# Selective scan in a Trainium2 kernel: one state's input tile of sixteen moved from TensorE to VectorE

## The chip, the core and the metric

The kernel runs on one core of one Trainium2 chip. The metric is the device time of one execution in microseconds (us). The core's engines have queues of their own and work side by side; they wait for one another with semaphores: TensorE (PE in the profile, its weight loads are PEld), VectorE (DVE), ScalarE (ACT), GpSimd (POOL) and SyncE (SP), which issues the DMA transfers. TensorE writes only to PSUM; VectorE and ScalarE can reach PSUM, GpSimd works in SBUF.

## The reference, cut

The program is four layers deep (a Mamba layer with a selective scan, a gated expert layer, a second Mamba-like mixer, a quantised feed-forward layer), with layer norms and residuals between them. The change touches the scan of the first:

```python
def _selective_scan(x, dt, A, Bm, Cm):        # 4 sequences, 1024 channels, 256 steps, 16 states
    def step(h, inp):
        x_t, dt_t, B_t, C_t = inp
        dA = jnp.exp(dt_t[..., None] * A)
        dBx = dt_t[..., None] * B_t[:, None, :] * x_t[..., None]
        h = dA * h + dBx
        y = jnp.einsum('bdn,bn->bd', h, C_t)
        return (h, y)
```

For each state n, h is a first-order recurrence over time with decay exp(dt.A[n]) and input dt.x.B[n]; y is the sum over n of h.C[n]. B and C are the same for all channels.

## The kernel before, in words

`selective_scan` (from L472) lays channels on the 128 partitions and time on the free axis. A unit is one state n of a "pair": two tiles of 128 channels (`a` = 0, 1) by one half of the tokens (512, two sequences), so 1024 elements a partition. There are 2 halves x 4 pairs x 16 states = 128 units; unit i is pair `kk` = i // 16 and state `n` = i % 16. For each unit:

- ScalarE, `decay(i)` (L540): da = exp(dt.A[n]), two instructions of 510 columns. Two buffers: it waits for scan i-2 (`s_h`).
- TensorE, `inputs(i)` (L669): the tile dt.x.B[n] into a PSUM buffer `dbx[i % 2]`. B[n] varies with time, which lies on the free axis. So u = dt.x is turned once a pair (`turn`, L648; `copied`, L551, takes it to SBUF as `uT`), and eight 128x128 matmuls of `uT` with a diagonal matrix of B[n] (`diag`) turn it back and scale it. It waits for scan i-2.
- VectorE, `scan(i)` (L600): the recurrence, from da (SBUF) and dbx (PSUM), into one of three buffers `hh`. It waits for da, dbx and for GpSimd's product i-3.
- GpSimd (L635 on): pr = h.C[n], with C[n] a row that was broadcast to all partitions (`crow`, four states a DMA, L529). It waits for scan i, and for `summed(i-3)`, which frees its buffer.
- TensorE, `summed(i)` (L690): eight transposes of pr that add up in PSUM `zT`. It waits for the product i.

TensorE's queue is written out by hand (L702 on): in iteration i it holds `inputs(i+2)`, then `turn(kk+1)` at n = 10, then `summed(i-2)`, then `turn_back(kk-1)` at n = 5. ScalarE's queue is `decay(i)`, and after it `summed_out(kk-1)` at n = 4 (copies zT to u), `copied(kk+1)` at n = 13 and, in pair 3, `narrow_diag` (L564), which makes the diagonal of the second half. `summed(0)` of the next pair starts zT anew and so waits for `summed_out`. VectorE's queue is the scans in order, with `skip(kk-1)` (L608) behind scan 8 and `dt_x(kk+1)` (L592, u = dt.x) behind scan 9. The first diagonals are made by `wide_diag` (L514), four by VectorE and six by GpSimd, the last six by ScalarE.

SyncE sends the C rows to DRAM in `scan_front` (L287) and loads them broadcast in `selective_scan` (L524 to L529), for the second half when the last pair of the first half has used them.

Of the kernel before, what the change touches and what calls it, by code (L numbers as in the profile page):

```python
# [15 lines left out]
F32 = mybir.dt.float32  # L16
F32R = mybir.dt.float32r
ALU = mybir.AluOpType
ACT = mybir.ActivationFunctionType
AX_X = mybir.AxisListType.X  # L20

P = 128
BATCH, SEQ, DM = 4, 256, 512
TOK = BATCH * SEQ
MT = TOK // P
KD = DM // P
HALF = 512
# [5 lines left out]
DIN, NST, RNK, TAPS = 1024, 16, 32, 4  # L33
CD = DIN // P
NX = RNK + 2 * NST
SCAN_EPS = 1e-6

NE, ER = 8, 16
# [44 lines left out]
def build(nc, I, out):  # L83

    with ExitStack() as top:
# [22 lines left out]

        x_tok = I["x"].rearrange("(m p) d -> p m d", p=P)
        out_tok = out.rearrange("(m p) d -> p m d", p=P)  # L110
        c_dram = nc.dram_tensor("c_rows", [NST, TOK], F32, kind="Internal").ap()
        acs_dram = nc.dram_tensor("acs_rows", [NHEAD, TOK], F32, kind="Internal").ap()
        tab_dram = nc.dram_tensor("step_tables", [NG, P, 3 * MT * 2 * PAIRS], F32, kind="Internal").ap()
        x_dram = nc.dram_tensor("x_kept", [TOK, DM], F32, kind="Internal").ap().rearrange("(m p) d -> p m d", p=P)
# [116 lines left out]
def scan_front(nc, sem, sb, banks, I, xT, xc, sz, dt, bt, cst, eps, c_dram, o):  # L231

    R = RNK + 2 * NST
# [3 lines left out]
    with ExitStack() as c:  # L237
# [33 lines left out]
        with nc.Block() as block:  # L271
            @block.sync
            def _(sp):
                def load(s):
                    if s >= 2:
                        sp.wait_ge(s_lo, s - 1)
                    sp.dma_start(ws[s % 2][:], I["w_in0"][s]).then_inc(s_w[s % 2], 16)

                load(0)
                load(1)  # L280
                for t, n in ((cw, "conv_w0"), (cb, "conv_b0"), (xp, "x_proj"), (dp, "dt_proj"), (db, "dt_bias0"),
                             (lw, "ln_w0")):
                    sp.dma_start(t[:], I[n]).then_inc(s_tab, 16)
                for s in range(2, CD):
                    load(s)
                sp.wait_ge(s_bcn, 2)
                sp.dma_start(c_dram, bcn[RNK + NST:R, :]).then_inc(s_out, 16)  # L287
                sp.wait_ge(s_out, 16)

            @block.gpsimd  # L290
            def _(pool):
# [180 lines left out]
def selective_scan(nc, sem, sb, banks, I, xc, dt, o, bt, ident, c_dram):  # L472
# [8 lines left out]
    BR = 4  # L481
    with ExitStack() as c:
        crow = sb(c, "ss_c", [P, NST, HALF])
        diag = sb(c, "ss_diag", [P, NST, TB, P])
        na = sb(c, "ss_na", [P, CD, NST])
        dd = sb(c, "ss_d", [P, CD])
        u = sb(c, "ss_u", [P, 2, HALF])
# [13 lines left out]
        s_zs, s_zt = sem("ss_zT_copied"), sem("ss_z_turned_back")  # L501
        s_dbx, s_da, s_h, s_pr, s_y, s_fin = (sem("ss_dbx_ready"), sem("ss_decay"), sem("ss_h_ready"), sem("ss_prod"),
                                              sem("ss_summed"), sem("ss_done"))
        V_FIRST, P_FIRST = 4, 10
        two = lambda t: t.rearrange("p (a t) -> p a t", a=2)

        def tokens(kk):
            half = kk // PR
# [4 lines left out]

        def wide_diag(eng, n):  # L514

            return eng.tensor_tensor(diag[:, n], ident.unsqueeze(1).to_broadcast([P, TB, P]),
                                     bt[:, 0:TB, n].unsqueeze(2).to_broadcast([P, TB, P]), ALU.mult)

        with nc.Block() as block:
            @block.sync  # L520
            def _(sp):
                sp.dma_start(na[:], I["a_log0"]).then_inc(s_in, 16)
                sp.dma_start(dd[:], I["d_0"]).then_inc(s_in, 16)
                for half in range(NH):  # L524
                    for r0 in range(0, NST, BR):
                        if half:
                            sp.wait_ge(s_pr, UNITS // NH - NST + r0 + BR)
                        src = c_dram[r0:r0 + BR, half * HALF:(half + 1) * HALF]
                        sp.dma_start(crow[:, r0:r0 + BR, :], src.partition_broadcast(P)).then_inc(s_c[r0 // BR], 16)  # L529

            @block.scalar
            def _(act):
# [18 lines left out]
                def copied(kk):  # L551
                    act.wait_ge(s_ut, kk + 1)
                    if kk >= 2:
                        act.wait_ge(s_dbx, (kk - 1) * NST)
                    for a in range(2):
                        act.activation(uT[kk % 2][:, a].rearrange("p m d -> p (m d)"), tz[:, a * HALF:(a + 1) * HALF],
                                       ACT.Copy).then_inc(s_us, 1)

                def summed_out(kk):
                    act.wait_ge(s_y, (kk + 1) * NST)  # L560
                    for a in range(2):
                        act.activation(u[:, a, :], zT[:, a * HALF:(a + 1) * HALF], ACT.Copy).then_inc(s_zs, 1)

                def narrow_diag(half, n):  # L564
                    for m in range(TB):
                        ins = act.activation(diag[:, n, m, :], ident, ACT.Copy,
                                             scale=bt[:, half * TB + m, n:n + 1])
                    ins.then_inc(s_dact, 1)

# [5 lines left out]
                for i in range(2, UNITS):  # L575
                    kk, n = divmod(i, NST)
                    decay(i)
                    if n == OUT_AT and kk:
                        summed_out(kk - 1)
                    if n == TURN_AT + 3 and kk + 1 < KB:  # L580
                        copied(kk + 1)
                    if kk == PR - 1:
                        act.wait_ge(s_dbx, i + 1)
                        narrow_diag(1, n)
                summed_out(KB - 1)

# [1 line left out]
            def _(dve):  # L588
# [3 lines left out]
                def dt_x(kk):  # L592
                    if kk >= 2:
                        dve.wait_ge(s_zt, kk - 1)
                    elif kk:
                        dve.wait_ge(s_ut, kk)
                    dve.tensor_tensor(u[:], dt[:, tiles(kk), tokens(kk)], xc[:, tiles(kk), tokens(kk)], ALU.mult
                                      ).then_inc(s_u, 1)

                def scan(i):  # L600
                    dve.wait_ge(s_da, i + 1)
                    dve.wait_ge(s_dbx, i + 1)
                    if i >= RH:
                        dve.wait_ge(s_pr, i - RH + 1)
                    dve.tensor_tensor_scan(hh[i % RH], da[i % 2][:], dbx[i % 2][:], 0.0, ALU.mult, ALU.add  # L605
                                           ).then_inc(s_h, 1)
# [9 lines left out]

                dt_x(0)
                for n in range(V_FIRST):
                    wide_diag(dve, n).then_inc(s_dv, 1)
                dve.wait_ge(s_in, 32)  # L620
                for i in range(UNITS):
                    kk, n = divmod(i, NST)
                    scan(i)
                    if n == SKIP_AT and kk:
                        skip(kk - 1)
                    if n == TURN_AT - 1 and kk + 1 < KB:
                        dt_x(kk + 1)
# [19 lines left out]
            def _(pe):  # L647
# [20 lines left out]

                def inputs(i):  # L669
                    kk, n = divmod(i, NST)  # L670
                    if i >= 2:
                        pe.wait_ge(s_h, i - 1)
                    if kk == 0:
                        if n < V_FIRST:
                            pe.wait_ge(s_dv, n + 1)
                        elif n < P_FIRST:
                            pe.wait_ge(s_dp, n - V_FIRST + 1)
                        else:
                            pe.wait_ge(s_dact, n - P_FIRST + 1)
                    if kk == PR:  # L680
                        pe.wait_ge(s_dact, NST - P_FIRST + n + 1)
                    for a in range(2):
                        if n == 0:
                            pe.wait_ge(s_us, 2 * kk + a + 1)
                        for m in range(TB):
                            ins = pe.matmul(dbx[i % 2][:, a * HALF + m * P:a * HALF + (m + 1) * P], uT[kk % 2][:, a, m, :],  # L686
                                            diag[:, n, m, :], start=True, stop=True)
                    ins.then_inc(s_dbx, 1)

                def summed(i):  # L690
# [1859 lines left out]
```

## Time and profile before

| | |
|---|---|
| median of 3 runs | 2571.89 us (2567.72 to 2571.96) |
| the profiled execution | 2572.07 us, its span 2570.3 us |
| busy in the span | PE 2378.4, PEld 1923.2, DVE 1840.6, ACT 1504.5, POOL 1213.2 us |
| L605, the scans | 128, 291.5 us busy, 2283 ns each |
| L686, `inputs` | 2048 matmul records (16 a unit), 253.7 us busy |
| L642, the products by C | 128, of 2401 and 2395 ns mean |
| L597, `dt_x` | 8, 12.4 us busy, 1547 ns each |

The scan stage runs from the first scan at 187.1 us to the last at 546.8 us. All times in the rows are microseconds from the start of the span, a row's duration is its second number. The releaser in brackets is what ended the idle time of the engine before the row. Each `inputs` is 8 matmul instructions and shows as 16 records of loads and of matmuls, each `summed` as 8. PEclk is the granted clock of TensorE, 1.00 at 2.4 GHz and 0.50 at 1.2 GHz. Starts and ends of neighbouring rows can overlap by some hundredths, since ends are modelled.

### The profile page before, as it was taken

The page shows a single profiled execution, that of the slowest core. Times are in us where ns is not written, and L with a number is a line of the kernel's source. Part 1 is how long each engine was busy: PE and PEld are TensorE (multiplying, and loading weights), DVE is VectorE, ACT ScalarE, POOL GpSimd, SP SyncE. Part 2 cuts the span into 40 slices and gives each one's busy share as a digit, 9 for nine tenths or more (in the row PEclk, how much of TensorE's full clock was granted, in tenths as well). Part 3 has the DMA queues.
Part 4 walks back from the last instruction along what each step waited for, and adds up shares of the span by engine and source line. Part 5 has one row for each costly group of instructions (what it writes and reads, how often), then busy time and mean ns, then how long its engine had stood idle before and what let it go on. Part 6 is the DMA issues. An engine that isn't in the chain of part 4 may idle for free. (4 is left out here: it accounts for less than half of the span.)

```text
span 2570.3 us, 38269 instructions
## 1 busy us (share of the span) xinstructions
PE 2378.4 (93%) x13836; PEld 1923.2 (75%) x13836; DVE 1840.6 (72%) x3052; ACT 1504.5 (59%) x3201; POOL 1213.2 (47%) x782
## 2 busy tenths in 40 slices
PE   5979999977659999999999999999999999779997
PEld 4559999976446777777777777777777777569996
DVE  4558888874537866866866966857857857597777
ACT  2355584553327966956956857867857768632221
POOL 1228888864224643633634625724625535432212
PEclk9989999988869999999999999999999999889999
DMA  2010020021022412322312312313312213201100
GB/s 83 26 61 7 1 66 2 1 70 34 30 86 88 124 58 79 110 65 77 119 50 80 113 54 92 97 58 99 94 60 96 87 62 99 92 25 50 41 35 34
DMA packets 108541, 167.42 MB, mean 65 GB/s; under 512 B 9489, under 2 KB 77457, under 8 KB 107329
## 3 DMA queue, kind: packets, MB, share of 16 engines
q1 hardware_dynamic: 108352, 164.97, 20.2%
q8 instruction: 111, 1.82, 0.3%
q14 instruction: 78, 0.63, 0.1%
HBM read 158.58 MB, written 6.36 MB: 64 GB/s over the span
## 5 line engine op out<-in xcount | busy, mean ns | idle before, releaser
L78 PE MATMUL mg_pb<-xTh,mg_wh 128*128 128x512 f32 x1152 | 479.5, 416 | 16.7 <-POOL mg_wl L1525 16.7
L1535 POOL TENSOR_TENSOR mg_y<-mg_hT,mg_sg 128x512 f32<-128x512 f32 x128 | 187.8, 1467 | 598.2 <-DVE mg_hT L1771 598.2
L79 PE MATMUL mg_pb<-xTl,mg_wh 128*128 128x512 f32 x1152 | 453.7, 394 | 0.0
L80 PE MATMUL mg_pb<-xTh,mg_wl 128*128 128x512 f32 x1152 | 452.3, 393 | 0.0
L1719 DVE SCALAR_TENSOR_TENSOR mg_hT<-mg_pb,mg_cw,mg_hT 128x510 f32<-128x510 f32 (+2 forms) x432 | 318.8, 742 | 31.4 <-ACT mg_hT L1891 22.7
L605 DVE TENSOR_TENSOR_SCAN o<-ss_da,ss_dbx 128x1024 f32<-128x1024 f32 x128 | 291.5, 2283 | 53.6 <-PE ss_dbx L686 48.9
L1746 DVE TENSOR_TENSOR mg_m<-mg_gb,mg_cb 128x384 f32<-128x384 f32 x512 | 265.7, 550 | 71.6 <-ACT mg_gb L1941 68.2
L78 PEld LDWEIGHTS mg_pb<-xTh,mg_wh 128*128 128x128 f32 x1152 | 217.3, 189 | 75.9 <-issue 19.2
L686 PE MATMUL ss_dbx<-ss_diag,ss_uT 128*128 128x128 f32 x2048 | 253.7, 278 | 8.6 <-DVE o L605 7.6
L548 ACT ACTIVATE ss_da<-dt,ss_na 128x510 f32<-128x510 f32 x256 | 170.3, 714 | 146.3 <-DVE o L605 146.1
L80 PEld LDWEIGHTS mg_pb<-xTh,mg_wl 128*128 128x128 f32 x1152 | 217.2, 189 | 51.3
L686 PEld LDWEIGHTS ss_dbx<-ss_diag,ss_uT 128*128 128x128 f32 x2048 | 241.7, 194 | 11.2 <-DVE o L605 10.0
L79 PEld LDWEIGHTS mg_pb<-xTl,mg_wh 128*128 128x128 f32 x1152 | 218.0, 189 | 38.5
L642 POOL TENSOR_TENSOR ss_pr<-o,ss_c 128x1024 f32<-128x1024 f32 x86 | 206.4, 2401 | 37.1 <-PE ss_zT L697 34.5
L1941 ACT ACTIVATE mg_gb<-mg_nd 128x256 f32<-128x256 f32 x512 | 189.8, 371 | 54.7 <-DVE mg_nd L1764 54.7
L1935 ACT ACTIVATE mg_gb<-mg_abc,mg_tabs 128x128 f32<-128x128 f32 x512 | 183.3, 358 | 22.8 <-DVE mg_m L1746 21.7
L1525 POOL TENSOR_TENSOR mg_wl<-mg_ws,mg_wh 128x1024 fp32r<-128x1024 f32 x72 | 177.5, 2465 | 6.0
L78 PE MATMUL mg_tb<-mg_wogh,mg_yh 128*128 128x512 f32 x448 | 180.0, 402 | 0.0
L79 PE MATMUL mg_tb<-mg_wogl,mg_yh 128*128 128x512 f32 x448 | 177.1, 395 | 0.0
L80 PE MATMUL mg_tb<-mg_wogh,mg_yl 128*128 128x512 f32 x448 | 177.0, 395 | 0.0
L1621 PE MATMUL mg_py<-mg_m,mg_hc 128*64 128x256 f32 x1024 | 165.6, 402 | 9.6 <-DVE mg_m L1746 9.5
L1795 DVE SCALAR_TENSOR_TENSOR o<-mg_tb,mg_rs,o 128x512 f32<-128x512 f32 x56 | 41.8, 747 | 179.5 <-PE mg_tb L80 179.5
(321 smaller groups left out, 5387.3 us busy)
## 6 DMA issues: line engine op xcount, KB each, us to landing
mg_abc<-acs_rows SPq DMA_DIRECT2D x256, 256.0 KB, 3.4
mg_ws<-in_w_in SPq DMA_DIRECT2D x72, 512.0 KB, 3.6
mg_wos<-in_w_out SPq DMA_DIRECT2D x64, 256.0 KB, 3.7
ss_c<-c_rows SPq DMA_DIRECT2D x8, 1024.0 KB, 5.7
ff_ws<-in_w SPq DMA_DIRECT2D x7, 1024.0 KB, 4.8
x<-in_x SPq DMA_DIRECT2D x16, 256.0 KB, 4.2
ip_ws<-in_w_in SPq DMA_DIRECT2D x8, 512.0 KB, 3.5
ff_w2s<-in_w SPq DMA_DIRECT2D x7, 512.0 KB, 5.8
```

Source lines behind the costliest of these rows:

```text
L78: pe.matmul(out, lhs[0], rhs[0], start=start, stop=False)
L79: pe.matmul(out, lhs[0], rhs[1], start=False, stop=False)
L80: return pe.matmul(out, lhs[1], rhs[0], start=False, stop=stop)
L605: dve.tensor_tensor_scan(hh[i % RH], da[i % 2][:], dbx[i % 2][:], 0.0, ALU.mult, ALU.add).then_inc(s_h, 1)
L642: pool.tensor_tensor(pr[i % RP], two(hh[i % RH]), crow[:, n, :].unsqueeze(1).to_broadcast([P, 2, HALF]), ALU.mult).then_inc(s_pr, 1)
L686: ins = pe.matmul(dbx[i % 2][:, a * HALF + m * P:a * HALF + (m + 1) * P], uT[kk % 2][:, a, m, :], diag[:, n, m, :], start=True, stop=True)
L1525: pool.tensor_tensor(wl[s % 2][:], ws[:], wh[s % 2][:].bitcast(F32), ALU.subtract).then_inc(s_lo, 1)
L1535: pool.tensor_tensor(yb[:, p % RING, t], hT[s % 2][:, t], sg[s % 2][:, t], ALU.mult).then_inc(s_y2, 1)
L1719: i = dve.scalar_tensor_tensor(out=d3, in0=s3, scalar=w[:, TAPS - 1 - k:TAPS - k], in1=d3, op0=ALU.mult, op1=ALU.add)
L1746: dve.tensor_tensor(mm[u % 4][:], gb[u % 2][:, 0:BLK], cbt[:, u // 2, :], ALU.mult).then_inc(s_m, 1)
L1935: act.activation(gb[u % 2][:, 2 * P:BLK], abc[(BATCH * p + b) % 3][:, hh, P:SEQ], ACT.Exp, bias=tabs[g % 2][:, 2, 2 * b, 2 * q + hh:2 * q ...
L1941: act.activation(gb[u % 2][:, 0:2 * P], nd[u % 4][:], ACT.Exp, scale=1.0 if by_dve(p, b) else -1.0).then_inc(s_e, 1)
```

## The change

State 2 of each pair (`BY_DVE`) gets its tile from VectorE. VectorE multiplies u (dt.x, still in SBUF and not turned) by a row of B[2] that is broadcast to all partitions (`brow`), and writes the product into the same PSUM buffer that TensorE would have used. The instruction is queued behind scan 0 of the pair; it waits for that scan, and in pairs 0 and 4 for the row's DMA. `scan(2)` waits for it. TensorE's `inputs` returns at once for state 2 and the other 15 states stay as they are, with their counts of semaphores moved (`at`, `by_pe`). There is one diagonal fewer. SyncE writes one more row to DRAM in the front, and loads `brow` ahead of the C rows of each half. `summed_out` waits for the product too, since it overwrites u.

```diff
+BY_DVE = 2
-                sp.dma_start(c_dram, bcn[RNK + NST:R, :]).then_inc(s_out, 16)
-                sp.wait_ge(s_out, 16)
+                sp.dma_start(c_dram[0:NST, :], bcn[RNK + NST:R, :]).then_inc(s_out, 16)
+                sp.dma_start(c_dram[NST:NST + 1, :], bcn[RNK + BY_DVE:RNK + BY_DVE + 1, :]).then_inc(s_out, 16)
+                sp.wait_ge(s_out, 32)
...
-        diag = sb(c, "ss_diag", [P, NST, TB, P])
+        diag = sb(c, "ss_diag", [P, NST - 1, TB, P])
+        brow = sb(c, "ss_b", [P, HALF])
-        V_FIRST, P_FIRST = 4, 10
+        V_FIRST, P_FIRST = 5, 10
+        def at(n):
+            return n if n < BY_DVE else n - 1
+        def by_pe(i):
+            kk, n = divmod(i, NST)
+            return kk * (NST - 1) + at(n)
...
                 for half in range(NH):
+                    if half:
+                        sp.wait_ge(s_dbv, PR)
+                    src = c_dram[NST:NST + 1, half * HALF:(half + 1) * HALF]
+                    sp.dma_start(brow[:], src.partition_broadcast(P).rearrange("p a n -> p (a n)")).then_inc(s_b, 16)
...
                 def summed_out(kk):
                     act.wait_ge(s_y, (kk + 1) * NST)
+                    act.wait_ge(s_dbv, min(kk + 2, KB))
...
-                    if kk == PR - 1:
-                        act.wait_ge(s_dbx, i + 1)
+                    if kk == PR - 1 and n != BY_DVE:
+                        act.wait_ge(s_dbx, by_pe(i) + 1)
                         narrow_diag(1, n)
...
+                def inputs(kk):
+                    i = kk * NST + BY_DVE
+                    dve.wait_ge(s_h, i - 1)
+                    if kk % PR == 0:
+                        dve.wait_ge(s_b, 16 * (kk // PR + 1))
+                    dve.tensor_tensor(two(dbx[i % 2][:]), u[:], brow[:].unsqueeze(1).to_broadcast([P, 2, HALF]), ALU.mult
+                                      ).then_inc(s_dbv, 1)
                 def scan(i):
+                    kk, n = divmod(i, NST)
                     dve.wait_ge(s_da, i + 1)
-                    dve.wait_ge(s_dbx, i + 1)
+                    if n == BY_DVE:
+                        dve.wait_ge(s_dbv, kk + 1)
+                    else:
+                        dve.wait_ge(s_dbx, by_pe(i) + 1)
...
                 for n in range(V_FIRST):
-                    wide_diag(dve, n).then_inc(s_dv, 1)
+                    if n != BY_DVE:
+                        wide_diag(dve, n).then_inc(s_dv, 1)
...
                     scan(i)
+                    if n == BY_DVE - 2:
+                        inputs(kk)
...
                 def inputs(i):
                     kk, n = divmod(i, NST)
+                    if n == BY_DVE:
+                        return
                     if i >= 2:
                         pe.wait_ge(s_h, i - 1)
```

## Rows read from the trace of the kernel before

**Rows 1.** Busy time by stretch: length, PE, PEld, DVE, ACT, POOL busy, clock, DMA
```profile
280.00:325.00 45.00, 44.46 (x402) 44.22 (x401) 38.75 (x20) 22.87 (x38) 38.49 (x16) 1.00 0.00 1
```

**Rows 2.** Waits of the scan stage: engine and line, waited for, us, times, longest
```profile
DVE o L605 <- PE ss_dbx L686: 48.9, 94, 1.6
```

**Rows 3.** Timeline at the second pair's start: start, duration, instruction, idle before
```profile
234.13 2.29 DVE L605 TENSOR_TENSOR_SCAN o<-ss_da,ss_dbx 128x1024 f32<-128x1024 f32 x1 [0.37 <-PE ss_dbx L686]
234.64 1.86 PEld L686 LDWEIGHTS ss_dbx<-ss_diag,ss_uT 128*128 128x128 f32 x16
...
235.06 2.36 POOL L642 TENSOR_TENSOR ss_pr<-o,ss_c 128x1024 f32<-128x1024 f32 x1 [0.29 <-PE ss_zT L697]
236.42 0.91 PEld L697 LDWEIGHTS ss_zT<-cst,ss_pr 128*128 128x128 f32 x8
...
236.79 2.29 DVE L605 TENSOR_TENSOR_SCAN o<-ss_da,ss_dbx 128x1024 f32<-128x1024 f32 x1 [0.38 <-PE ss_dbx L686]
...
239.96 1.86 PEld L686 LDWEIGHTS ss_dbx<-ss_diag,ss_uT 128*128 128x128 f32 x16
...
243.01 1.06 ACT L562 ACTIVATE ss_u<-ss_zT 128x512 f32<-128x512 f32 x2
...
244.40 0.91 PEld L697 LDWEIGHTS ss_zT<-cst,ss_pr 128*128 128x128 f32 x8
```

**Rows 4.** Timeline around `dt_x` of the first, second and third pair
```profile
214.78 2.36 POOL L642 TENSOR_TENSOR o<-o,ss_c 128x1024 f32<-128x1024 f32 x1 [0.33 <-PE ss_zT L697]
...
216.03 2.19 DVE L597 TENSOR_TENSOR ss_u<-dt,xc 128x1024 f32<-128x1024 f32 x1
...
218.14 6.76 DVE L605 TENSOR_TENSOR_SCAN o<-ss_da,ss_dbx 128x1024 f32<-128x1024 f32 x3
...
220.47 1.86 PEld L686 LDWEIGHTS ss_dbx<-ss_diag,ss_uT 128*128 128x128 f32 x16 [0.78 <-DVE o L605]
...
259.90 2.36 POOL L642 TENSOR_TENSOR ss_pr<-o,ss_c 128x1024 f32<-128x1024 f32 x1 [0.32 <-PE ss_zT L697]
...
261.98 1.36 DVE L597 TENSOR_TENSOR ss_u<-dt,xc 128x1024 f32<-128x1024 f32 x1
...
262.53 3.02 POOL L642 TENSOR_TENSOR ss_pr<-o,ss_c 128x1024 f32<-128x1024 f32 x1 [0.27 <-PE ss_zT L697]
...
307.10 1.36 DVE L597 TENSOR_TENSOR ss_u<-dt,xc 128x1024 f32<-128x1024 f32 x1
```

**Rows 5.** Groups by line and shape: busy us, mean ns, idle before
```profile
L430 DVE TENSOR_TENSOR dt<-dt,sp_rl 128x1024 f32<-128x1024 f32 x4 | 4.6, 1219 | 0.0
```

**Rows 6.** Timeline in the fourth pair: ScalarE's copy and the transposes behind it
```profile
334.71 1.05 ACT L562 ACTIVATE ss_u<-ss_zT 128x512 f32<-128x512 f32 x2
...
335.87 0.86 PEld L697 LDWEIGHTS ss_zT<-cst,ss_pr 128*128 128x128 f32 x8 [1.15 <-POOL o L642]
```

**Rows 7.** TensorE after holes: timeline; then stretches (length, PE busy, clock, DMA)
```profile
196.75 3.39 PEld L686 LDWEIGHTS ss_dbx<-ss_diag,ss_uT 128*128 128x128 f32 x16 [3.27 <-DVE o L605]
...
605.11 0.66 PE L849 MATMUL op_tb<-cst,o 128*128 128x128 f32 x4 [2.61 <-DVE o L958]
...
819.86 0.63 PE L1604 MATMUL mg_tb<-cst,mg_hT 128*128 128x128 f32 x4 [2.37 <-DVE mg_hc L1737]
...
2292.37 0.81 PE L2184 MATMUL tl_px<-cst,o 128*128 128x128 f32 x4 [2.59 <-DVE xT3l L2374]
...
605.00:610.00 5.00, 4.89 (x17) 0.66 0.00 0
...
819.80:824.00 4.20, 4.14 (x25) 1.00 0.72 233
...
2292.30:2296.50 4.20, 4.13 (x22) 0.59 0.00 0
```

**Rows 8.** Timeline of the first pair: VectorE's first four scans
```profile
187.10 4.46 DVE L605 TENSOR_TENSOR_SCAN o<-ss_da,ss_dbx 128x1024 f32<-128x1024 f32 x2 [0.80 <-PE ss_dbx L686]
...
194.41 4.46 DVE L605 TENSOR_TENSOR_SCAN o<-ss_da,ss_dbx 128x1024 f32<-128x1024 f32 x2 [2.85 <-ACT ss_da L548]
```

More of the change, by code:

```diff
@@ L110, in build @@
         out_tok = out.rearrange("(m p) d -> p m d", p=P)
-        c_dram = nc.dram_tensor("c_rows", [NST, TOK], F32, kind="Internal").ap()
+        c_dram = nc.dram_tensor("c_rows", [NST + 1, TOK], F32, kind="Internal").ap()
         acs_dram = nc.dram_tensor("acs_rows", [NHEAD, TOK], F32, kind="Internal").ap()
@@ L503, in selective_scan @@
                                               sem("ss_summed"), sem("ss_done"))
-        V_FIRST, P_FIRST = 4, 10
+        V_FIRST, P_FIRST = 5, 10
+        s_b, s_dbv = sem("ss_b_in"), sem("ss_dbx_by_dve")
         two = lambda t: t.rearrange("p (a t) -> p a t", a=2)
+        def at(n):
[3 more added lines that the diff above has]
+            return kk * (NST - 1) + at(n)
         def tokens(kk):
@@ L514, in wide_diag @@
         def wide_diag(eng, n):
-            return eng.tensor_tensor(diag[:, n], ident.unsqueeze(1).to_broadcast([P, TB, P]),
+            return eng.tensor_tensor(diag[:, at(n)], ident.unsqueeze(1).to_broadcast([P, TB, P]),
                                      bt[:, 0:TB, n].unsqueeze(2).to_broadcast([P, TB, P]), ALU.mult)
@@ L553, in copied @@
                     if kk >= 2:
-                        act.wait_ge(s_dbx, (kk - 1) * NST)
+                        act.wait_ge(s_dbx, by_pe((kk - 1) * NST))
                     for a in range(2):
@@ L565, in narrow_diag @@
                     for m in range(TB):
-                        ins = act.activation(diag[:, n, m, :], ident, ACT.Copy,
+                        ins = act.activation(diag[:, at(n), m, :], ident, ACT.Copy,
                                              scale=bt[:, half * TB + m, n:n + 1])
@@ L674, in inputs @@
                         if n < V_FIRST:
-                            pe.wait_ge(s_dv, n + 1)
+                            pe.wait_ge(s_dv, at(n) + 1)
                         elif n < P_FIRST:
@@ L680, in inputs @@
                     if kk == PR:
-                        pe.wait_ge(s_dact, NST - P_FIRST + n + 1)
+                        pe.wait_ge(s_dact, NST - P_FIRST + at(n) + 1)
                     for a in range(2):
@@ L686, in inputs @@
                             ins = pe.matmul(dbx[i % 2][:, a * HALF + m * P:a * HALF + (m + 1) * P], uT[kk % 2][:, a, m, :],
-                                            diag[:, n, m, :], start=True, stop=True)
+                                            diag[:, at(n), m, :], start=True, stop=True)
                     ins.then_inc(s_dbx, 1)
```

## The prediction, made before the changed kernel was built or run

> **What bounds the kernel now.** I read the busy time by stretch first. In the scan stage (about 187 to 547 us of the span) TensorE is busy 44.46 of 45 us, VectorE 38.75 and GpSimd 38.49 [rows 1]. The view of waits agrees: VectorE's scan waits 48.9 us in 94 places for TensorE's dt.x.B tile [rows 2]. Then the timeline of one pair's start, to see who is late at which unit. Below, "unit n" is state n of the second pair; its scans start at 234.13 and 236.79, so the beat is 2.66 us [rows 3]. TensorE fills it: the eight matmuls of `inputs` (16 records) take 236.42 - 234.64 = 1.78 us of weight loads, the eight transposes of `summed` the other 0.88 [rows 3]. VectorE's scan takes 2.29. So TensorE is the bound by throughput, by 0.37 us a unit. But look also at the order: `inputs(n+2)` waits for scan n and stands ahead of `summed(n-2)` in TensorE's queue. Scan 1 ends at 236.79 + 2.29 = 239.08, `inputs(3)` starts at 239.96 [rows 3]. That 0.88 us is all the room the dependency has.
>
> **What the change removes.** In each of 8 pairs TensorE no longer makes the tile of unit 2: 8 x 1.78 = 14.2 us of a full engine. This would be the gain if TensorE could go on with something else. It can't: with `inputs(2)` gone, the queue holds `summed(-3)` (236.42), `summed(-2)` (237.30), then `inputs(3)`, which still waits for scan 1; `summed(-1)` is queued behind it. TensorE's queue is empty at 238.18, its last transpose ends at about 238.44, and it waits.
>
> **What it adds.** One VectorE product (128x1024, both inputs in SBUF, output in PSUM) between scan 0 and scan 1. Scan 0 ends at 234.13 + 2.29 = 236.42, and its own wait for that scan lets it go no earlier. The same kind of product, `dt_x`, shows what it meets. At 216.03 it was issued while GpSimd's product of 214.78 to 217.14 ran; it took 2.19 us and ended at 218.22, 1.08 after GpSimd's end. At 261.98 it ended at 263.34, again 1.08 after GpSimd's (259.90 + 2.36 = 262.26); and the next GpSimd product, started at 262.53 inside it, took 3.02 in place of 2.36, so 0.66 longer [rows 4]. So the two engines take turns over whole instructions. For unit 2 GpSimd's product of 235.06 to 237.42 is always under way when scan 0 ends [rows 3]. The new product therefore ends at 237.42 + 1.08 = 238.50. No row shows VectorE writing a 128x1024 product to PSUM, so I bound it: alone and to SBUF it takes 1.22 [rows 5], which would end it at 237.6 if PSUM output freed it from the turns; the upper end is half a microsecond on top, as the spread from 1.22 to `dt_x`'s mean of 1.55 and some more for PSUM. I take 238.50, as `dt_x` has the same two SBUF inputs.
> The page "SBUF — State Buffer" of the Trainium skill, section "Who interferes with whom", puts the conflict on the two SBUF inputs and does not exempt a PSUM output; no row here shows that case.
>
> **What is late next.** A scan starts 0.08 before the modelled end of a product (263.26 against 263.34; the first of the rows 4 group's scans the same), so scan 1 starts at 238.42 instead of 236.79. TensorE resumes 2.33 after such a scan's start (218.14 to 220.47, [rows 4]): `inputs(3)` starts at 240.75 instead of 239.96, that is +0.79, after 240.75 - 238.44 = 2.31 us of idle TensorE. Scan 2 follows scan 1 (three scans in 6.76 us), scan 3 has its tile 2.15 after `inputs(3)` starts (234.64 to 236.79) and its decay before that. From there TensorE is again the bound with its old beat, so nothing gives the 0.79 back in the pair. The 1.78 saved turns into idle time, and a little more. The displaced GpSimd product ends at about 240.7, just as scan 1 does, and covers nothing else: `summed` of it is queued for 245. Pair 1 to 7: 7 x 0.79 = 5.5 us.
>
> ScalarE is next in line. `summed_out` (243.01, 1.06 us) leads TensorE's `summed(0)` at 244.40 by little [rows 3]; it follows `decay(4)`, which waits for scan 2. Scan 2 now ends at about 242.95; decay to 244.29, `summed_out` from 244.19, and TensorE follows 1.16 after its start (334.71 to 335.87, [rows 6]): 245.35, against 245.19 at which TensorE would be free. So +0.16 more where TensorE runs at full speed. The new wait in `summed_out` for the product is over long before.
>
> **The clock.** The new 2.31 us hole comes once a pair. In the trace there are six holes of 2.37 to about 2.7 us in front of TensorE work that started at the full level (605.11 the first, 2292.37 the last). After five of them the granted clock fell: 0.66 in 605 to 610, 0.59 in 2292 to 2296; after 819.86 (2.37 us of idle) it stayed at 1.00 in 820 to 824 [rows 7]. The price in this very stage is at 196.75: after 3.27 us without a load (3.08 without a matmul), 16 loads took 3.39 us instead of 1.86, at the 1.2 GHz level, so 1.53 us, once, until the clock is back at 2.4 [rows 7]. By the nearest row (2.37) none of seven pairs would fall, by the five of six all would fall; I take four: 4 x 1.53 = 6.1 us, and the 0.16 counts in the other three, 0.5 us.
> The page "TensorE: Matmul & The Clock Gate" of the Trainium skill, section "Why this matters for your kernels", asks only for no idle gaps above about 3 us. By it a hole of 2.31 costs no clock and the time would be that of the first rival; five of the six holes here speak against it.
>
> **The first pair** is apart. Scans run at 187.10 and 194.41 (in twos), the second pair of them held up by ScalarE's tables [rows 8], so the product lies in a hole. If VectorE gets its turn before GpSimd's first product, which waits for the same scan, scan 1 ends near 192.9, `inputs(3)` is early enough, and the clock's dip, which before fell on `inputs(4)`, falls where it costs less: -1.5. If GpSimd is first, scan 1 ends near 195.1 and `inputs(3)` with it: up to +0.5. I take -0.5. GpSimd makes five wide diagonals instead of six, VectorE four as before; both are done before the first scan.
>
> **At nothing:** the 256 KB row of B is loaded first of the stage's rows and wanted only after the scan of 187.10; its reload for the second half waits for the product of pair 3 and is wanted 45 us later; the row of B written to DRAM in the front joins a transfer that ends long before the stage. Left out in pair 3 is one narrow diagonal of ScalarE, which is not the bound there. If the cover of the load is gone, the first pair pays one wait of a few us.
>
> **Sum.** The profiled execution's own time is 2572.07 (span 2570.3 and 1.8 around it), 0.2 above the median of 2571.89. 2572.07 + 5.5 + 6.1 + 0.5 - 0.5 = 2583.7. I take 2583.5.
>
> **Rivals.** (1) The clock stays up. All else as above: 2572.07 + 5.5 + 7 x 0.16 - 0.5 = 2578.2. For it: the hole of 2.37 that was harmless. Against: the other five.
> (2) The new product isn't held by GpSimd, because it writes PSUM. Then it ends at 237.6, scan 1 starts at 237.5, and `inputs(3)` comes at 239.9: no shift, a hole of 1.5 us, clock mostly up: 2570 to 2574. Against: both `dt_x` rows.
> (3) Faster: TensorE's throughput decides. 8 x 1.78 = 14.2 less: 2557.8. It decides only if scan 1 ends before 238.2, where TensorE runs out; since scan 1 takes 2.24 start to start after the product, the product would have to take no time at all, and at 1.22 the gain is 0.06 a pair. Only an `inputs(3)` that need not wait for scan 1 would do it, and the code has the wait.
> (4) Slower still: the write to PSUM costs 0.5 us more (+3.5 in seven pairs), and the clock falls in all seven (+4.6 over the sum less the 0.5): near 2591.
>
> **How the numbers follow.** My forecast (delay plus some falls of the clock, 2579 to 2588) has 0.55, rival 1 (2576 to 2579) 0.19, rival 2 0.15, rival 3 0.04, rival 4 0.07. The range from 2573 to 2590 leaves out rival 3, about half of rival 2 and part of rival 4. A difference of 0.2% is 5.1 us, about what a measurement of this kernel can tell from none; that puts the line at 2577.0. Slower by more: 0.55 + 0.07 + 0.11 of rival 1 = 0.73. Within: 0.08 of rival 1 and 0.14 of rival 2 = 0.22. Faster: 0.05.
>
> **What the profile after should show.** The new VectorE product takes 2.1 to 2.2 us in pairs 1 to 7 and ends 1.08 after a GpSimd product; the GpSimd product after it takes about 3 us; TensorE waits about 2.3 us for L605's scan once a pair; scan 2 comes 1.2 later after scan 0 than before; seven pairs grow from 45.12 us (261.98 to 307.10, [rows 4]) to 45.9 or to 47.4, the latter with a granted clock under 1.00 behind the hole. TensorE's matmul records are 128 fewer and its busy time falls, the span does not. It is wrong if the product is short, if scan 1 follows scan 0 within 3.6 us, or if TensorE shows no hole.

## The result, and the profile after

| | before | changed |
|---|---|---|
| median | 2569.22 us (2566.66 to 2571.96, 6 runs) | 2581.30 us (2580.31 to 2589.47, 6 runs) |
| ratio | | 1.0053, 95% interval 1.0041 to 1.0064 |
| profiled execution | 2572.07 us | 2589.47 us |
| TensorE matmul records | 13836 | 13708 |

The changed kernel is 12.1 us slower, with 128 matmul records fewer. The forecast was 2583.5, which is 11.6 over the median it started from.

The profiled execution of the changed kernel is the longest of its six. The others took 2580.31 to 2582.32. The mean granted clock over the whole execution is 0.958 in the profiled one and 0.961 to 0.963 in the others. A second profile of the same kernel, below, shows where such a difference can lie.

The timeline at the second pair's start, in the changed kernel (start, duration, instruction, idle before); it answers to [rows 3]. L634 is the scan, L622 the new product, L674 GpSimd's product, L720 `inputs`, L731 `summed`, L579 `summed_out`:

```profile
234.62 2.29 DVE L634 TENSOR_TENSOR_SCAN o<-ss_da,ss_dbx 128x1024 f32<-128x1024 f32 x1 [0.37 <-PE ss_dbx L720]
235.13 1.86 PEld L720 LDWEIGHTS ss_dbx<-ss_diag,ss_uT 128*128 128x128 f32 x16
...
235.55 2.36 POOL L674 TENSOR_TENSOR ss_pr<-o,ss_c 128x1024 f32<-128x1024 f32 x1 [0.30 <-PE ss_zT L731]
...
236.94 2.06 DVE L622 TENSOR_TENSOR ss_dbx<-ss_u,ss_b 128x1024 f32<-128x1024 f32 x1
...
237.90 1.04 PE L731 MATMUL ss_zT<-cst,o 128*128 128x128 f32 x8
238.23 2.96 POOL L674 TENSOR_TENSOR ss_pr<-o,ss_c 128x1024 f32<-128x1024 f32 x1 [0.32 <-PE ss_zT L731]
238.91 4.45 DVE L634 TENSOR_TENSOR_SCAN o<-ss_da,ss_dbx 128x1024 f32<-128x1024 f32 x2
...
241.24 3.07 PEld L720 LDWEIGHTS ss_dbx<-ss_diag,ss_uT 128*128 128x128 f32 x16 [2.55 <-DVE o L634]
241.24 3.36 PE L720 MATMUL ss_dbx<-ss_diag,ss_uT 128*128 128x128 f32 x16 [2.31 <-DVE o L634]
...
244.69 2.29 DVE L634 TENSOR_TENSOR_SCAN o<-ss_da,ss_dbx 128x1024 f32<-128x1024 f32 x1 [1.33 <-PE ss_dbx L720]
```

GpSimd's product runs from 235.55 to 237.91. VectorE's is issued at 236.94 and ends at 239.00, 1.09 after it. Scan 1 starts 4.29 after scan 0 instead of 2.66. TensorE's last transpose ends at 238.94, then it is idle for 2.31 us; such an idle time is called a hole here. When it resumes, 16 loads take 3.07 us instead of 1.86, and scan 3 comes late by that.

The stretches behind two of these holes, and the one between them (length, TensorE busy, granted clock, DMA share, GB/s); they answer to [rows 1, 7]:

```profile
241.20:246.00 4.80, 4.76 (x28) 0.64 0.00 0
246.00:288.70 42.70, 39.93 (x359) 1.00 0.01 1
288.80:293.50 4.70, 4.70 (x27) 0.64 0.00 0
```

The waits of the scan stage (engine and line, waited for, us in total, times, longest):

```profile
DVE o L634 <- PE ss_dbx L720: 52.0, 80, 1.6
...
PE ss_dbx L720 <- DVE o L634: 24.7, 16, 4.2
```

and in the kernel before:

```profile
PE ss_dbx L686 <- DVE o L605: 7.6, 9, 3.1
```

Before, VectorE waited 48.9 us for TensorE [rows 2] and TensorE 7.6 us in 9 places for VectorE. Now TensorE waits 24.7 us, in 16 places. Both engines wait for each other, in turns.

The best ruler for this stage is the distance between two `dt_x` in succession, one pair. In the kernel before it is 45.12 us (261.98 to 307.10, [rows 4]); the next, up to the `dt_x` in pair 3, where ScalarE makes the second half's diagonals, is 46.30 (307.10 to 353.40). In the changed kernel's profile they are 47.55 and 47.97:

```profile
264.90 1.36 DVE L614 TENSOR_TENSOR ss_u<-dt,xc 128x1024 f32<-128x1024 f32 x1
...
312.45 1.35 DVE L614 TENSOR_TENSOR ss_u<-dt,xc 128x1024 f32<-128x1024 f32 x1
...
360.42 1.36 DVE L614 TENSOR_TENSOR ss_u<-dt,xc 128x1024 f32<-128x1024 f32 x1
```

So a pair costs 2.43 more, and pair 3 costs 1.67 more. Seven pairs are 7 x 2.43 - 0.76 = 16.3 us. The first pair is unchanged (28.99 against 28.93 from the first scan to `dt_x`). From the first scan's start to the last scan's end the stage took 378.33 us against 361.98, so 16.35 more, which is the same sum. The span grew by 17.3.

### The profile page after: what moved, and what is told of

Its sections match the earlier page's. It is cut to its first block and busy times, and to the rows that moved or that the text cites. A ratio compares the mean times of both kernels' runs of the same rounds, so it can differ in the third digit from the quotient of the medians.

```text
span 2587.6 us, 38029 instructions
## 1 busy us (share of the span) xinstructions
PE 2381.8 (92%) x13708; PEld 1923.6 (74%) x13708; DVE 1853.7 (72%) x3060; ACT 1503.6 (58%) x3197; POOL 1217.4 (47%) x781
## 5 line engine op out<-in xcount | busy, mean ns | idle before, releaser
L634 DVE TENSOR_TENSOR_SCAN o<-ss_da,ss_dbx 128x1024 f32<-128x1024 f32 x128 | 290.7, 2281 | 55.5 <-PE ss_dbx L720 52.0
L720 PE MATMUL ss_dbx<-ss_diag,ss_uT 128*128 128x128 f32 x1920 | 247.0, 284 | 25.6 <-DVE o L634 24.7
L720 PEld LDWEIGHTS ss_dbx<-ss_diag,ss_uT 128*128 128x128 f32 x1920 | 234.6, 199 | 29.8 <-DVE o L634 28.6
L674 POOL TENSOR_TENSOR ss_pr<-o,ss_c 128x1024 f32<-128x1024 f32 x86 | 210.5, 2449 | 47.9 <-PE ss_zT L731 43.4
```

What stands on the lines that cost most here:

```text
L674: pool.tensor_tensor(pr[i % RP], two(hh[i % RH]), crow[:, n, :].unsqueeze(1).to_broadcast([P, 2, HALF]), ALU.mult).then_inc(s_pr, 1)
```

## The experiments

Two theories stood against each other, apart from single terms. **H, hole and clock:** the new product delays scan 1, `inputs(3)` and all that follows by about 0.9 us a pair, the saved 1.78 us of TensorE turn into idle time, and that idle time lowers the clock behind it. **D, delay only:** the clock does not matter; or, its opposite, **T:** TensorE's throughput decides and the gain is lost in something accidental. "A pair" below is the distance of two `dt_x` in the profiled execution (45.12 before), and "hole" is TensorE's idle time ahead of `inputs(3)`. Ratios are to the kernel before, measured beside each group of kernels on the same chip. Its medians were 2569.39 us for the first four rows of the table, 2568.14 for the next four and 2569.48 for the last four.

Pairs are the sharper measure. The scan stage does not begin at the same time in every execution: in seven of the fourteen profiled ones the first scan starts at 183.0 to 184.4 us, in the other seven at 186.9 to 188.1, and the changed kernel is in both groups. Two medians that differ by 2 or 3 us can differ by that alone.

| kernel | hole, us | pair, us | clock low behind | median us | ratio, 95% interval |
|---|---|---|---|---|---|
| changed, again | 2.31 | 46.00 or 47.55 | 5 of 7 | 2581.40 | 1.0054 (1.0041 to 1.0066) |
| hole filled, 8 matmuls | 0.53 | 45.99 | 0 of 7 | 2573.84 | 1.0018 (1.0009 to 1.0028) |
| one SBUF input | 1.54 | 45.22 | 0 of 7 | 2568.65 | 1.0001 (0.9993 to 1.0010) |
| no product | 0.69 | 44.36 | 0 of 7 | 2563.11 | 0.9975 (0.9967 to 0.9984) |
| product added only | 0.53 | 45.99 | 0 of 7 | 2573.78 | 1.0019 (1.0011 to 1.0028) |
| order, one place | 1.44 | 45.99 | 0 of 7 | 2575.02 | 1.0025 (1.0015 to 1.0035) |
| the same, summed_out earlier | 1.44 | 45.42 | 0 of 7 | 2570.69 | 1.0006 (0.9996 to 1.0016) |
| hole filled, 2 matmuls | 1.87 | 47.55 | 7 of 7 | 2581.53 | 1.0051 (1.0038 to 1.0064) |
| hole filled, 3 matmuls | 1.64 | 45.98 | 0 of 7 | 2573.83 | 1.0021 (1.0010 to 1.0031) |
| GpSimd waits | 1.49 | 45.69 | 0 of 7 | 2572.35 | 1.0012 (1.0003 to 1.0021) |
| order everywhere | 1.49 | 44.92 | 0 of 7 | 2564.17 | 0.9982 (0.9973 to 0.9991) |
| its control, no change | none | 44.96 | 0 of 7 | 2566.44 | 0.9989 (0.9978 to 1.0000) |

### The changed kernel again

No edit.

> The changed kernel itself, once more, on the chip of the next three. Theory H (hole and clock): TensorE waits 2.31 us once a pair for scan 1, because the product of VectorE lies between scan 0 and scan 1; this delays inputs(3) by 0.79 us in pairs 1 to 7 (5.5 us in all), and the rest of the loss is the granted clock that falls behind the hole, about 1.6 us each time. How many of the seven pairs it hits differs from execution to execution: the profiled one had all seven and 2589.5, the other five 2580.3 to 2582.3. H expects 2578 to 2590 here, mean clock lower where the time is longer, and about 0.45% over the kernel before. Rival D (delay only: the clock has nothing to do with the time, all 12 us are the product and the waits): the same time, but no relation between clock and time.

Measured: 2580.32 to 2586.08, median 2581.40. Its profiled execution (2580.45) had the low clock behind five of seven holes. Rows of TensorE behind three holes of the same length (timeline), then two of the stretches (length, busy, clock, DMA):

```profile
236.23 3.53 PE L720 MATMUL ss_dbx<-ss_diag,ss_uT 128*128 128x128 f32 x16 [2.32 <-DVE o L634]
...
283.61 3.68 PE L720 MATMUL ss_dbx<-ss_diag,ss_uT 128*128 128x128 f32 x16 [2.31 <-DVE o L634]
...
379.68 2.05 PE L720 MATMUL ss_dbx<-ss_diag,ss_uT 128*128 128x128 f32 x16 [2.31 <-DVE o L634]
...
236.20:240.50 4.30, 4.27 (x25) 0.63 0.00 0
379.70:384.00 4.30, 4.30 (x38) 1.00 0.39 84
```

The same hole is followed by the low clock in one place and by the full clock in another. Pairs whose hole is followed by the low clock take 47.55 us, the two that are not take 46.00. That gives both terms from one profile: 46.00 - 45.12 = 0.88 is the delay, 47.55 - 46.00 = 1.55 the clock. D is out.

What decides for a given pair is open. DMA traffic does not: of the two holes that were spared, one lies beside transfers (share 0.39, above) and one does not (473.20 to 478.00: clock 1.00, DMA 0.00), and in the first profile the hole before 384.32 was followed by 0.64 with a DMA share of 0.35.

The two profiles of this kernel also show how far the clock behind the holes explains the spread of its times. Their spans are 2587.6 and 2578.6 us, 9.0 apart. Of this, 4.2 lie ahead of the first scan (it starts at 187.53 and at 183.35; between 110 and 130 us the granted clock is 0.83 in the first and 1.00 in the second), 3.6 in the scan stage (378.33 against 374.72), of which the two spared pairs are 3.1, and 1.2 behind it. So only a third is the clock behind the holes. How many pairs it hit in the executions without a profile isn't known.

### TensorE's hole filled with work of no use

```diff
                     if n == BY_DVE:
+                        for m in range(8):
+                            pe.matmul(tz[:, m * P:(m + 1) * P], uT[kk % 2][:, 0, m % TB, :], ident, start=True, stop=True)
                         return
```

> The changed kernel; in the place of the removed inputs(2) TensorE runs eight matmuls of the same size with the unit matrix into a PSUM tile (ss_tz) that is free at that point, and nobody reads them. The output stays the reference's. The hole is then 2.31 - 1.78 = 0.5 us. The delay stays: scan 1 ends as late as in the changed kernel. H expects no lower clock behind the pairs, seven pairs of 45.12 + 0.95 us, so about 6 us over the kernel before (0.25%) and 5 to 6 us under the changed kernel, though TensorE does as much as before the change. Rival D expects the changed kernel's time or more (+12 us over before).

Measured: +4.5 us to before, and 7.6 under the changed kernel. TensorE does the 14.2 us of work again that the change had taken from it, and the kernel gets faster. The hole is 0.53 us, each pair 45.99 (0.87 over before) and pair 3 0.79 over:

```profile
235.57 2.05 PE L723 MATMUL ss_dbx<-ss_diag,ss_uT 128*128 128x128 f32 x16 [0.53 <-DVE o L634]
...
257.66 1.35 DVE L614 TENSOR_TENSOR ss_u<-dt,xc 128x1024 f32<-128x1024 f32 x1
...
303.65 1.35 DVE L614 TENSOR_TENSOR ss_u<-dt,xc 128x1024 f32<-128x1024 f32 x1
```

The clock is at 1.00 through the stage. By the profile the scan stage is 4.2 us longer than before (366.21): 6.0 in seven pairs, less 1.8 in the first pair, which takes 27.13 us from its first scan to `dt_x` in place of 28.93. VectorE and GpSimd stand as in the changed kernel.

### The added product alone

```diff
+                def inputs(kk):
+                    dve.wait_ge(s_h, kk * NST + BY_DVE - 1)
+                    ...
+                    dve.tensor_tensor(two(tz[:]), u[:], crow[:, 0, :].unsqueeze(1).to_broadcast([P, 2, HALF]), ALU.mult
+                                      ).then_inc(s_dbv, 1)
...
                     scan(i)
+                    if n == BY_DVE - 2:
+                        inputs(kk)
```

> The kernel before, with TensorE's work whole, and one product added on VectorE behind scan 0 of each pair: u by row 0 of the C rows (same size, two SBUF inputs, output to the PSUM tile ss_tz, which nobody reads at that point). The output stays the reference's. It is the added half of the change alone. H: scan 1 starts as late as in the changed kernel (4.3 us after scan 0), inputs(3) comes 0.79 us late, TensorE waits only 0.8 us there, the clock stays up, and the time is that of the kernel with the filled hole, 4 to 6 us over before. If the removal of TensorE's work gave anything back in the changed kernel, this one would be 14 us slower than before.

Measured: +5.6 us, pair 45.99, the hole 0.53. It is the same kernel in time as the one with the hole filled (2573.78 and 2573.84). So the added half of the change costs 0.87 us a pair. The removed half gives nothing back: where the clock stays up, a pair of the changed kernel takes 46.00 (above), so with TensorE's matmuls there or not, `inputs(3)` comes when scan 1 has ended.

### Turns with GpSimd, or the write to PSUM

```diff
-                    dve.tensor_tensor(two(dbx[i % 2][:]), u[:], brow[:].unsqueeze(1).to_broadcast([P, 2, HALF]), ALU.mult
+                    dve.tensor_scalar(two(dbx[i % 2][:]), u[:], dd[:, 0:1], 0.0, ALU.mult, ALU.add
```

> The changed kernel; VectorE's product of u and the B row is replaced by u times one number per partition, same size and same PSUM output, so with one SBUF input in place of two (this leaves B of state 2 out, the output is not the reference's). Tells the turns with GpSimd from the cost of writing PSUM. H (turns because of two SBUF inputs): the instruction takes 1.2 us and starts no later than scan 0's end, GpSimd's product behind it keeps 2.36 us, scan 1 starts 3.44 after scan 0, TensorE's hole is 1.46 us, inputs(3) comes 0.06 us earlier than in the kernel before, the clock does not fall, the time is that of the kernel before within 2 us. Rival P (the write to PSUM is what makes it 2.06 us): it stays at 2 us, and the time at +10 us or more.

Measured: 2568.65, ratio 1.0001. The groups by line of the new product (count | busy us, mean ns | idle before, us), first in this kernel:

```profile
L622 DVE TENSOR_SCALAR ss_dbx<-ss_u,ss_d 128x1024 f32<-128x1024 f32 x8 | 10.3, 1287 | 0.3
```

in the changed kernel:

```profile
L622 DVE TENSOR_TENSOR ss_dbx<-ss_u,ss_b 128x1024 f32<-128x1024 f32 x8 | 15.7, 1958 | 0.3
```

in the kernel where GpSimd waits (below):

```profile
L622 DVE TENSOR_TENSOR ss_dbx<-ss_u,ss_b 128x1024 f32<-128x1024 f32 x8 | 9.9, 1234 | 0.3
```

and from the timeline of the kernel with one input, GpSimd's product beside it:

```profile
233.37 2.35 POOL L674 TENSOR_TENSOR ss_pr<-o,ss_c 128x1024 f32<-128x1024 f32 x1 [0.32 <-PE ss_zT L731]
```

This kernel leaves B of state 2 out. With one SBUF input the instruction takes 1.29 us on average beside GpSimd's product, and that keeps 2.35. With two and GpSimd idle it takes 1.23, to the same PSUM tile. So the write to PSUM costs 0.01 us over SBUF ([rows 5] had 1.22), and of the 2.06 us 0.83 are the wait for GpSimd. The wait costs 0.87 - 0.10 = 0.77 us a pair (45.99 against 45.22), and it is what stretches the hole from 1.54 to 2.31.

### No product at all

```diff
-                    dve.tensor_tensor(two(dbx[i % 2][:]), u[:], brow[:]..., ALU.mult
+                    dve.tensor_scalar(dbx[i % 2][:, 0:4], u[:, 0, 0:4], dd[:, 0:1], 0.0, ALU.mult, ALU.add
```

> The changed kernel; the product is cut to 4 columns of one SBUF input (this leaves the tile of state 2 out, the scan of state 2 reads an old tile, the output is not the reference's). What is left is the pure gain from taking 14.2 us of work from TensorE. H (TensorE's queue is held by scan 1, which itself can't start before its own tile is there, 2.66 us after scan 0): inputs(3) comes at most 0.84 us earlier than in the kernel before, the rest of the 1.78 is idle, and ScalarE's summed_out takes back 0.2 of it in six pairs: 4 to 6 us faster than the kernel before, with a hole of 0.7 us. Rival T (TensorE's throughput is what counts): 14.2 us faster.

This kernel leaves the tile of state 2 out. Measured: 6.3 us faster than before, a pair 44.36, so 0.76 less. That is as much as the removed 1.78 us a pair are worth when the replacement is free. Scan 1 starts as before, because its own tile is the limit, and then TensorE waits 0.69:

```profile
237.25 0.22 DVE L622 TENSOR_SCALAR ss_dbx<-ss_u,ss_d 128x4 f32<-128x4 f32 x1
...
237.59 6.77 DVE L633 TENSOR_TENSOR_SCAN o<-ss_da,ss_dbx 128x1024 f32<-128x1024 f32 x3
...
239.93 2.05 PE L719 MATMUL ss_dbx<-ss_diag,ss_uT 128*128 128x128 f32 x16 [0.69 <-DVE o L633]
```

T is out: it asked for 14.2 us. The saving is 6.3 in time, a little over the 4 to 6 of H, and 5.4 by pairs (6 x 0.76 and 0.84 in pair 3), within it.

### Real work into the hole

```diff
+                    first = n == BY_DVE - 1 and kk
+                    if first:
+                        summed(i - LAG)
                     if i + LEAD < UNITS:
                         inputs(i + LEAD)
...
-                    if LAG <= i:
+                    if LAG <= i and not first:
                         summed(i - LAG)
```

> The changed kernel with TensorE's queue in another order in one place: summed(-1), that is the transposes of the last unit of the pair before, ahead of inputs(3). H: 0.88 us of real work moves into the hole, which shrinks to 1.4 us, so the clock stays up: 6 us less than the changed kernel. inputs(3) itself comes no earlier, and inputs(4), which could come 0.44 us earlier, gives that back because summed(0) waits for ScalarE's summed_out: 4 to 6 us over before. If the order were worth its 0.88 in each pair besides the clock, it would be at the kernel before.

> As e4_order, and ScalarE's summed_out one unit earlier (behind decay 3 in place of decay 4). H: summed(0) no longer waits; what is left of the delay is scan 2's end, 0.35 us a pair: 1 to 3 us over before, so within what can be told from it. Rival: ScalarE was not the limit and it is the same as e4_order.

The second has also `OUT_AT` 3 in place of 4. Measured: +6.9 us and +2.6 us. The hole is 1.44 in both and the clock stays up. The first has the pair of the filled hole, 45.99: the 0.88 us that were moved into the hole gain nothing themselves. With ScalarE's copy one unit earlier a pair is 45.42, 0.30 over before, where 0.35 was expected for scan 2's end; in pair 3 it is 45.42 too, against 46.30 before. So ScalarE was the next limit in the reordered kernel.

### How long a hole costs the clock

```diff
-                        for m in range(8):
+                        for m in range(2):
```

> As e1_fill8, but two matmuls (4 records, 0.45 us) into the hole in place of eight: the hole is about 1.86 us. The stretches of the trace before with holes of 1.98 us or less kept the full level, those of 2.6 lost it. H: few or none of the pairs lose the clock, and the time lies at that of e1_fill8 or up to 3 us over it. Rival: any hole costs in proportion to its length, and the time lies a quarter of the way from the changed kernel to e1_fill8, 2 us under the changed kernel.

> As e6_fill2, which with a hole of 1.87 us still had the lower clock behind all seven pairs of its profile, against what I expected; three matmuls (6 records, 0.67 us) leave a hole of 1.65 us. Holes of 1.44 and 1.54 us kept the clock up in all pairs. So this lies between: either the clock stays up and the time is that of e1_fill8, 4 to 7 us over before, or it falls and the time is 10 us or more over before.

Two matmuls missed the expectation: the hole of 1.87 us is followed by the low clock in all seven pairs of the profile, and the time is that of the changed kernel (2581.53). That profile is the longest of its five executions (2586.44, the others 2577.93 to 2581.86), so in the others fewer pairs may have been hit. Three matmuls leave 1.64 us, never followed by the low clock in the profile, and the time is that of the filled hole (2573.83). TensorE behind the holes of the one and of the other (timeline, then stretch):

```profile
238.06 3.37 PE L723 MATMUL ss_dbx<-ss_diag,ss_uT 128*128 128x128 f32 x16 [1.87 <-DVE o L634]
...
238.00:242.50 4.50, 4.44 (x25) 0.62 0.00 0
```
```profile
235.37 2.05 PE L723 MATMUL ss_dbx<-ss_diag,ss_uT 128*128 128x128 f32 x16 [1.64 <-DVE o L634]
...
235.30:240.00 4.70, 4.63 (x41) 1.00 0.00 0
```

One matmul more or less, 0.23 us of hole, goes with 7.7 us of time here. A cost in proportion to the hole is out. The length alone is no rule either. In the first pair, where TensorE has more and longer holes, a hole of 2.72 us left the clock at 1.00 in the kernel with three matmuls, and one of 3.14 us did so in the kernel with no product:

```profile
189.30 2.05 PE L723 MATMUL ss_dbx<-ss_diag,ss_uT 128*128 128x128 f32 x16 [2.72 <-DVE o L634]
```
```profile
192.77 2.05 PE L719 MATMUL ss_dbx<-ss_diag,ss_uT 128*128 128x128 f32 x16 [3.14 <-DVE o L633]
```

A next hole there, of 2.72 us, was followed by the low clock (0.57 in 197.50 to 200.00).

### GpSimd out of the way

First by a wait: GpSimd's product of unit 15 waits for the new product.

```diff
                     pool.wait_ge(s_h, i + 1)
+                    if n == NST - 1 and kk + 1 < KB:
+                        pool.wait_ge(s_dbv, kk + 2)
```

> The changed kernel; GpSimd's product of unit 15 (the one that was under way when VectorE's new product was issued) waits for the new product. Output stays the reference's. H (taking turns costs 0.85 us and makes the hole 2.31): the new product takes 1.2 us, scan 1 starts 3.4 to 3.5 us after scan 0, TensorE's hole is 1.5 us, which the runs with one SBUF input showed to leave the clock up. GpSimd then runs late by 2.6 us at that point, which ScalarE's summed_out passes on with some 0.3 us a pair: 0 to 3 us over before, 9 to 12 us under the changed kernel. Rival (GpSimd's delay is passed on whole): 5 us or more over before.

Measured: +2.9 us, 9.1 under the changed kernel. The product takes 1.23, the hole is 1.49, a pair 45.69. Of this 0.57 are over before, more than the 0.3 expected, because GpSimd is late and scan 2 waits for its buffer:

```profile
240.12 6.77 DVE L634 TENSOR_TENSOR_SCAN o<-ss_da,ss_dbx 128x1024 f32<-128x1024 f32 x3 [0.79 <-POOL ss_pr L676]
...
244.89 1.06 PE L733 MATMUL ss_zT<-cst,ss_pr 128*128 128x128 f32 x8 [0.37 <-ACT ss_u L579]
```

Then by order: `summed(i-2)` ahead of `inputs(i+2)` in every iteration, and `OUT_AT` 2, once in the changed kernel and once in the kernel before.

```diff
+                    if LAG <= i:
+                        summed(i - LAG)
                     if i + LEAD < UNITS:
                         inputs(i + LEAD)
                     if n == TURN_AT and kk + 1 < KB:
                         turn(kk + 1)
-                    if LAG <= i:
-                        summed(i - LAG)
```

> The changed kernel with TensorE's queue the other way round in every iteration, summed(i-2) ahead of inputs(i+2), and summed_out at n = 2. GpSimd then runs one beat earlier, right behind the scans, and has no product under way when VectorE issues the new one. H: the new product takes 1.2 us, GpSimd's next one 3 us or more, the hole is 1.5 us, filled by nothing, the clock stays up, the time is that of the kernel before within 2 us: even without the turns and the clock, the change gains nothing, because scan 0, product and scan 1 in a row take 5.7 us and TensorE's two beats were 5.3. Rival T (with the lock and the clock out of the way the saved 1.78 us a pair appear): 8 us or more faster than before.

> The control of e11_swap_all: the kernel before with the same two moves (summed ahead of inputs everywhere, summed_out at n = 2), TensorE making all 16 states. TensorE stays the bound with the same work, so H expects the time of the kernel before within 1.5 us.

Measured: 2564.17 (0.9982) with the change and 2566.44 (0.9989) without it. In the first, at the same place of the pair:

```profile
234.26 1.23 DVE L622 TENSOR_TENSOR ss_dbx<-ss_u,ss_b 128x1024 f32<-128x1024 f32 x1
...
234.31 3.39 POOL L674 TENSOR_TENSOR ss_pr<-o,ss_c 128x1024 f32<-128x1024 f32 x1 [0.29 <-DVE o L634]
...
235.41 6.77 DVE L634 TENSOR_TENSOR_SCAN o<-ss_da,ss_dbx 128x1024 f32<-128x1024 f32 x3
...
237.74 2.05 PE L720 MATMUL ss_dbx<-ss_diag,ss_uT 128*128 128x128 f32 x16 [1.49 <-DVE o L634]
```

Now GpSimd follows the scans directly; both engines are released by scan 0, VectorE is 0.05 us sooner and GpSimd waits instead. Both kernels missed their expectations: 5.3 us under before where "within 2" was expected, and 3.0 under where "within 1.5" was. The first is faster than both the kernel before and the changed one. But its control shows that this is mostly the order: by pairs 44.92 against 44.96, so the change itself is worth 0.04 us a pair here, and 0.85 in pair 3, where the control waits for ScalarE (44.93 against 45.78). The two intervals overlap. The control's own gain lies in three places: the first pair (27.15 us against 28.93), pair 3 (45.78 against 46.30) and 0.16 in each other pair. These 0.16 are the turns again: `dt_x` takes 1.20 us in both kernels in place of 1.36, because GpSimd's product now starts behind it, and the hole behind it is 0.39 in place of 0.55:

```profile
259.75 1.20 DVE L614 TENSOR_TENSOR ss_u<-dt,xc 128x1024 f32<-128x1024 f32 x1
...
259.92 3.25 POOL L674 TENSOR_TENSOR ss_pr<-o,ss_c 128x1024 f32<-128x1024 f32 x1 [1.13 <-DVE o L634]
```

## Why the prediction held, point by point

- **What bounds the kernel.** Right, with the distinction that mattered: TensorE is full (44.46 of 45, [rows 1]), but its queue is tied to the scans by two buffers with 0.88 us of room. The kernel with no product gained 0.76 of this and not 1.78.
- **The new product and GpSimd's turn.** Forecast to end 1.08 after GpSimd's product; 1.09 in the second pair, the product 2.06 to 2.07 in all seven pairs. The next GpSimd product is 2.96, as stretched as the one of [rows 4]. The open bound, a PSUM output that frees it or costs more, closed: it does neither (1.23 alone).
- **The delay.** Forecast +0.79 and a hole of 2.31; measured 2.31. In `inputs(3)`, 241.24 - 234.62 = 6.62 after scan 0, against 5.83 before, so 0.79.
- **ScalarE's 0.16.** Half of it: pairs at full clock are 0.87 to 0.88 over before, 0.08 beyond the 0.79. That ScalarE's copy is a limit is shown in the reordered kernel alone, where moving `summed_out` takes 0.57 away; in the changed kernel itself it wasn't moved.
- **The clock.** The direction was right and both sizes were a little off. The price is 1.55 (forecast 1.53). The count was forecast as four of seven; profiles show seven and five. By the first, the sum would be 3 x 1.55 higher, which meets the profiled execution to 1.1 us (2583.7 + 4.65 = 2588.4 against 2589.47). Four was a choice between none and all, with no row behind it, so that the sum came within 1 us of the measured difference (11.6 against 12.1) is in part luck. The choice of the nearest row (2.37, harmless, [rows 7]) as one end was of little use: the same hole of 2.31 went either way within one execution, and 1.87 went down seven times.
- **The first pair.** Forecast -0.5; in the changed kernel's profile +0.06. VectorE did get its turn first (189.85 against 189.90), but the dip of the clock took both `inputs(3)` and `inputs(4)`:

```profile
193.33 3.25 PE L720 MATMUL ss_dbx<-ss_diag,ss_uT 128*128 128x128 f32 x16 [4.16 <-DVE o L634]
...
197.15 3.77 PE L720 MATMUL ss_dbx<-ss_diag,ss_uT 128*128 128x128 f32 x16 [0.57 <-DVE o L634]
```

  In the second profile of the changed kernel the first pair is 0.8 shorter than before (28.15). In other kernels with a shorter hole there, it is 1.8 shorter (27.13 with the hole filled), so the -1.5 was in reach but not for this one.
- **At nothing.** No wait for the row of B shows in the changed kernel. The extra transfers were not run alone.
- **TensorE's busy time.** It was to fall, and it rose, from 2378.4 to 2381.8 us in the profile with all seven falls of the clock, with 128 records fewer: the records behind the holes take longer at 1.2 GHz. With one SBUF input, where the clock stays up, it is 2362.7.
- **Rival 1, clock stays up (2578.2).** It would have been the kernel with the hole filled, 4.5 us over before (6.1 forecast); out for this kernel. The page "TensorE: Matmul & The Clock Gate" of the Trainium skill, section "Why this matters for your kernels", allows gaps up to about 3 us. These runs do not agree with it: behind gaps of 1.87 and 2.31 us the clock was lower.
- **Rival 2, not held by GpSimd.** Out for this kernel, and its time about right where the hold was removed: forecast from 2 us under to 2 over the 2572.07 it started from, measured 0.7 under before with one input and 2.9 over with GpSimd waiting.
- **Rival 3, faster by 14.2.** Out. I wrote that a product of no time would be needed; even that gives 0.76 a pair.

## What to carry to other kernels

Taking work from the busiest engine pays only where the next thing in that engine's queue is ready. Here it waited for a scan that the replacement work itself had pushed back, so look for what ends last at the place of the edit, not at the busy share. A hole opened in TensorE's work can cost more than the delay that caused it (1.55 against 0.88 us here), and matmuls that nobody reads, or better transposes that are due anyway, win it back. Before giving VectorE a product of two SBUF tensors, see whether GpSimd is in one of its own at that moment: here the wait was 0.83 of 2.06 us, and moving GpSimd by a beat removed it. And measure inside the stage: the start of this stage alone moved by 4 us between executions.

## What the runs showed of the hardware that was not expected

- **The clock falls behind holes under 2 us.** In pairs 1 to 7, with TensorE otherwise full, the granted clock never fell behind holes of 0.53 to 1.64 us (0 of 7 pairs in each of nine profiles), behind 1.87 us it did in 7 of 7 (one profile), and behind 2.31 us in 7 of 7 and 5 of 7. The work after it is at 1.2 GHz and costs 1.55 us once. In the first pair, with more idle time around, holes of 2.72 and 3.14 us were spared. Why these and two of the seven were, was not settled.
- **VectorE writes PSUM as fast as SBUF:** a 128x1024 product of two SBUF inputs took 1.23 us to PSUM, 1.22 to SBUF.
- **The turns hold with an output in PSUM:** the product with two SBUF inputs waited for GpSimd's, the instruction with one did not (2.06 and 1.29 us). When one semaphore released both, VectorE was first in the rows read for it (189.85 against 189.90, 234.26 against 234.31), and at 234.31 GpSimd's product took 3.39 us.
